# Routed expert tiles: all transposes in a row and a down product over 128 rows; the third block's sums inside the last block

## The reference, cut to what matters

```
probs = softmax(x @ gate_w.T); the two best of 8 experts, weights renormed to 1
out   = silu(x @ shared_gate.T) * (x @ shared_up.T) @ shared_down.T       # inner width 352
g, u  = x @ expert_gate[e].T, x @ expert_up[e].T                          # inner width 176, per expert
y     = silu(g) * u @ expert_down[e].T
out  += sum over the two chosen experts of weight * y
x     = x + s * silu(out)                                                 # s: result of the time mix
```

## Time and profile before

| what | us |
|---|---|
| median of 3 runs | 929.03 |
| lowest, highest | 928.94, 964.37 |
| the profiled execution | 927.84 |
| its span | 926.0 |
| PE, DVE, ACT, POOL busy | 836.1, 688.6, 521.7, 358.9 |

### The profile page before, as it was taken

How to read it: one execution, slowest core, us unless ns; L and a number is a source line. 1 busy time by engine, 2 the same in 40 slices (tenths; PEclk the granted TensorE clock), 3 DMA queues, 4 the chain that set the end, 5 groups by cost and what they waited for, 6 DMA issues and landing times. The chain is left out here.

```text
span 926.0 us, 18081 instructions
## 1 busy us (share of the span) xinstructions
PE 836.1 (90%) x6672; PEld 532.8 (58%) x6672; DVE 688.6 (74%) x1023; ACT 521.7 (56%) x955; POOL 358.9 (39%) x294
## 2 busy tenths in 40 slices
PE   3999999999999999989999999995689899999994
PEld 3853333333333333333587887985576578888883
DVE  5889899999999999981266666578985665444376
ACT  4321687787778778877642335436482334555442
POOL 5430355347445743576002000017956641334300
PEclk9975799999999999999999999996965799999998
DMA  6595123222222222000192000001051231333252
GB/s 224 205 252 186 23 52 59 52 51 50 49 50 49 49 49 49 16 15 20 41 269 3 1 1 12 1 1 56 5 214 64 81 74 47 109 109 108 93 166 69
DMA packets 59511, 69.97 MB, mean 76 GB/s; under 512 B 24768, under 2 KB 46400, under 8 KB 59040
## 3 DMA queue, kind: packets, MB, share of 16 engines
q1 hardware_dynamic: 55272, 58.28, 23.9%
q0 software_dynamic: 3408, 9.38, 2.8%
q10 hardware_dynamic: 744, 1.15, 0.4%
HBM read 40.06 MB, written 26.62 MB: 72 GB/s over the span
## 5 line engine op out<-in xcount | busy, mean ns | idle before, releaser
L671 ACT ACTIVATE probs_t<-psum 128x512 f32<-128x512 f32 x512 | 272.0, 600 | 111.0 <-PE psum L771 108.4
L685 DVE TENSOR_REDUCE row_max<-psum 128x1 f32<-128x1024 f32 x256 | 299.4, 1216 | 16.9 <-PE psum L755 16.0
L612 POOL TENSOR_TENSOR lut_sum<-lut_sum,lut_tmp 128x1072 f32<-128x1072 f32 x60 | 150.9, 2516 | 172.1 <-DVE lut_tmp L710 171.4
L755 PE MATMUL psum<-KS,QS 48*128 48x512 f32 x512 | 188.2, 472 | 14.6 <-DVE row_max L685 13.6
L771 PE MATMUL psum<-QS,KS 50*128 50x512 f32 x512 | 199.5, 466 | 1.0 <-ACT probs_t L671 1.0
L771 PEld LDWEIGHTS psum<-QS,KS 50*128 50x128 f32 x512 | 84.8, 189 | 139.4 <-ACT probs_t L671 134.9
L783 PE MATMUL psum<-probs_t,VS 128*32 128x512 f32 x1024 | 143.1, 618 | 8.2 <-ACT o_sb L553 8.2
L755 PEld LDWEIGHTS psum<-KS,QS 48*128 48x128 f32 x512 | 83.0, 201 | 68.2 <-DVE row_max L685 60.5
L2267 POOL DMA_INDIRECT y_rows<-y_slot,ids x39 | 37.5, 962 | 82.6 <-ACT y_slot L2326 82.6
L710 DVE TENSOR_SCALAR lut_tmp<-lut_idx,lut 128x1072 f32<-128x1072 int32 x60 | 48.3, 806 | 10.1 <-POOL lut_sum L612 10.1
L783 PEld LDWEIGHTS psum<-probs_t,VS 128*32 128x32 f32 x1024 | 23.8, 108 | 45.6 <-ACT probs_t L671 36.5
(11 more groups left out here) (300 smaller groups left out, 1823.6 us busy)
## 6 DMA issues: line engine op xcount, KB each, us to landing
KS<-k_rows SPq DMA_DIRECT2D x31, 192.0 KB, 4.6
QS<-q_rows SPq DMA_DIRECT2D x31, 192.0 KB, 5.0
x_rows<-zero_rows SPq DMA_DIRECT2D x1, 4992.0 KB, 18.2
x_slot<-x_rows SPq DMA_DIRECT2D x39, 128.0 KB, 2.0
m_raw<-experts_w SPq DMA_DIRECT2D x2, 2432.0 KB, 12.2
q_rows<-part SPq DMA_DIRECT2D x8, 512.0 KB, 8.8
y_token<-y_rows SPq DMA_DIRECT2D x8, 512.0 KB, 7.8
x_tok<-x SPq DMA_DIRECT2D x4, 512.0 KB, 7.6
```

Of the source, the lines that this page charges most:

```text
L612: nc.gpsimd.tensor_tensor(wsum[:, c % 2, :], wsum[:, c % 2, :], wtmp[:, slot % 2, :], ALU.add).then_inc(lut_add, 1)
L671: nc.scalar.activation(pt[:, k % NPT, :], ring(k)[:], ACT.Exp, scale=float(E) ** -0.5).then_inc(p_ready, 1)
L685: nc.vector.tensor_reduce(mx[:, n % 2, col:col + 1], m.psum[:, 2 * (k % 2):2 * (k % 2) + 2, :], AX_XY, ALU.max).then_inc(max_done, 1)
L755: mm = nc.tensor.matmul(MX[k % 2][h][:], QS[n % NQK][rows(g, NROW), st * P:(st + 1) * P], KS[n % NQK][rows(g, NROW), h * BLK:(h + 1) * BLK ...
```

## The change

TensorE's routed iteration becomes `gate_up(i)`, `turn_h(i-1)`, `turn_x(i+2)`, `down_r(i-2)`. `down_r` sums over 128 rows in its second chunk too: the rows beyond 48 are zeros on both sides. In the last block `combine(2)` moves behind `product(3, 0)`, where `routed_sum` was, `routed_sum` moves behind `low_h(3, 0)`, ahead of `add_gated(1)`, and on ACT `gate_out(2)` moves ahead of `high(3, 2)`. Blocks 0 to 2 keep their order.

```diff
@@ ACT
                     silu(tb, c)
                     if c >= 1:
                         high(tb, c - 1)
+                    if c == NSC - 1 and tb == NB - 1:
+                        gate_out(tb - 1)
                 high(tb, NSC - 1)
...
-                else:
+                elif tb < NB - 1:
                     gate_out(tb - 1)
@@ DVE
                     if c == 0 and tb == NB - 1:
+                        combine(tb - 1)
+                    if c == 1 and tb == NB - 1:
                         routed_sum(tb)
                     if c == 1 and tb >= 2:
                         add_gated(tb - 2)
...
-                else:
+                elif tb < NB - 1:
                     combine(tb - 1)
@@ down_r
                 mm = three(nc, bank[6 + j % 2][:, 0:E],
-                           [(hth[0:n, j % 2, c, :], htl[0:n, j % 2, c, :],
-                             wh[0:n, bass.ds(e + 2 * KC * EI + c * E, E)], wl[0:n, bass.ds(e + 2 * KC * EI + c * E, E)])
-                            for c, n in ((0, P), (1, EI - P))])
+                           [(hth[:, j % 2, c, :], htl[:, j % 2, c, :],
+                             wh[:, bass.ds(e + 2 * KC * EI + c * E, E)], wl[:, bass.ds(e + 2 * KC * EI + c * E, E)])
+                            for c in range(2)])
@@ TensorE's loop
                     turn_h(i - 1)
+                if 0 <= i + 2 < NTL:
+                    turn_x(i + 2)
                 if 0 <= i - 2 < NTL:
                     down_r(i - 2, at_expert[i - 2])
-                if 0 <= i + 2 < NTL:
-                    turn_x(i + 2)
```

## The result

The changed kernel takes 916.94 us in the median of 5 runs (912.6 to 921.34), the kernel before 929.03 (5 runs by then). The ratio is 0.9858, with a 95% interval of 0.9823 to 0.9894: clear of no change, under 2%. 915 was forecast, with a range of 911.5 to 919. The profiled execution took 912.6, its span is 910.8.

The account below looks back on a forecast made before the run. TensorE's stream was taken to bound the loop, 2.458 us a tile against 2.11 of steps. Loop 12.5 plus end 0.5 gave 13.0 us off the profiled 927.84: 914.8, called 915, range 911.5 to 919.

Parts of the forecast that it names:

- The gaps: Routed loop: 128 rows remove 39 gaps of 0.19 and 38 of 0.14 us, 12.5 us; ends 10.4 and 13.6.
- register work: Routed loop: possible cause of the gaps, since the second product's weight addresses come from a register; no separate size or chance.
- The order: Routed loop: `turn_x` ahead of `down_r` costs nothing; 0.35 us a tile if the cover were gone.
- The end: Last block: reordering brings `add_shared` 1.7 us earlier, 0.5 if TensorE's clock falls; 0.5 taken.
- The fall of the clock: Last `down`s: TensorE's 2.9 us stand probably halves its clock for 3.2 us, losing 1.6 us.
- B: Routed loop: a new wait through ACT, DVE and TensorE leaves half the gain, 921 us; chance 0.07.
- C: Routed loop: the gap stays, only the tail's 0.5 us is gained, 927.3 us; chance 0.04.
- D: Routed loop: four transposes in a row lower TensorE's clock; 996 us if all tiles run so; chance 0.03.
- the two terms: Routed loop 12.5 us and last block 0.5 us, together a gain of 13.0 us.

Follow-up runs that it names:

- e1: Kernel before with only the second down product summed over all 128 rows; loop 91.58 us, ratio 0.9883.
- e2: Kernel before with only `turn_x` issued ahead of `down_r`, second product still 48 rows; loop 106.62 us, ratio 1.0042.
- e5: Changed kernel with the second down product summed over 64 rows instead of 128; loop 104.9 us, ratio 1.0006.
- e6: Changed kernel with the second down product summed over 96 rows instead of 128; loop 91.49 us, ratio 0.9839.
- e9: Changed kernel with a reordered end, plus the first layer's feed-forward last down product over 128 rows instead of 48; ratio 0.9848.
- e8: The changed kernel run again, unaltered, beside others on one chip; median 904.54 us, ratio 0.9861.
- e4: Changed kernel with 12 extra matmuls between the last block's `down(3,0)` and `down(3,1)`; median 915.05 us, ratio 0.985.

## Why the prediction was right

**The gaps.** The step that carried the forecast was that 0.19 and 0.14 us of each tile belong to the change between 48 and 128 rows. The measured gain of the loop, 12.2, is 0.3 under the 12.5 counted gap by gap, and within 10.4 to 13.6. e1 has it all, e2 none, and e5 and e6 put the border between 64 and 96 rows. The missing 0.3 can be placed. The sum let one product wait for DVE's low part, the very last, and took 0.2 off for it. The second last waits for it too:

```profile
854.73 0.42 DVE L2411 TENSOR_TENSOR ht_l<-psum,ht_h 128x256 fp32r<-128x256 f32 x1
855.30 0.38 PE L445 MATMUL psum<-m_h,ht_l 128*128 x1
```

DVE has `ht_l` ready at 855.15, and from the last matmul of the `down_r` before to the last of this one it is 1.29 us after the change (854.71 to 856.00) and was 1.29 before it (869.01 to 870.30): both gaps are gone there and a wait has taken their place.

That the feed-forward stage had the same gap with fixed addresses was the evidence against register work as its cause; e9 removed it there with the same cure, and e5 and e6 settle it in the loop.

**The order.** It was costed at nothing. e1 against the whole change, 91.58 and 91.50, bears that out with 128 rows. With 48 rows it would have cost: the rows behind the gap matter, 0.14 ahead of a transpose and 0.19 ahead of a matmul, which the prediction did not say for the order alone, though the expectation of e2 did.

**The end.** Both moves were sized right: `product(3,1)` 0.3 late, TensorE's stand 2.83 against 2.9 forecast, the gain 1.86 with the clock up (1.7 forecast). The fall of the clock was taken as likely from two stands of 2 to 2.5 us, and priced by the shorter stretch at half clock, 1.6 us: it cost TensorE 1.3 in this execution, and 0.75 was left where 0.5 was forecast; in e6 and e8 the tail of 14.53 leaves 0.54. Why the one stand loses the clock and the other keeps it, the rows of before could not say, and the runs do not either.

**The rivals.** B, a new wait in the loop: ACT and DVE kept up, and the period is the sum of TensorE's steps, up to the second last tile. C, the gap stays: refuted by e1. The rule cited for it (the Trainium skill, "TensorE: Matmul & The Clock Gate", Part 3, The mechanism), that a load overlaps running matmuls only where the row groups differ, does not fit the 0.12 steps of 128-row matmuls either. The prediction left out that the same section also lets a load into the background weight buffer be pulled ahead. D, the clock within the loop: 1.00 from 778 to 862, with four transposes in a row in every tile.

**What was luck.** The profiled execution came out at 912.6, below the 914.8 summed for it, because the code ahead of the loop happened to be 2.3 us faster in it. The median, 916.94, lies on the other side. The sum of the two terms came out to 0.1 us because their errors are of opposite sign: the loop gave 0.3 less, the end 0.25 more.

## What to carry to other kernels

Measure matmuls by the distance of their starts: an engine shown as busy throughout hid 0.34 us in 2.46. Where a product's last chunk has 48 or 64 rows beside chunks of 128, sum it over 128 rows with zeros if the rows can be had for nothing; 96 rows need no such care. When work is moved ahead of the instruction that feeds TensorE, count not only the wait but what TensorE's clock does in it, and put the work that nobody waits for behind the last instruction that TensorE needs.

## What the runs showed of the hardware

- A change between 48 or 64 rows and 128 costs 0.19 to 0.20 us each way between matmuls, and 0.14 from 48 rows into a transpose; between 96 and 128 it costs nothing.
- After a stand of 2.83 us the clock fell in four executions and stayed in one of the same order of work; after one of 1.88 us in the feed-forward stage it fell in four of twelve, after one of 1.5 us at that stage's end in five of twelve. After 1.1 and 0.8 us with four transposes between, at the loop's start, it fell in all eleven executions without extra matmuls; with eight extra matmuls there it stayed at 1.00, in one execution.
- Chips differ: the kernel before took 928.86, 916.96 and 928.61 us in the median on the three on which the experiments ran. The difference lies ahead of the loop: the copy of block 0's shared result starts at 760 to 764 in the four traces from the chip of 916.96 and at 769 to 776 in the others (e4 left out), while the changed kernel's loop takes 91.50 us in the first measurement and 91.58 in e8, and its middle blocks 27.8 in both. The ratio of the changed kernel did not differ: 0.9858 in the first measurement, 0.9861 on the chip of 916.96.
